# Four blocks of one-hots by one comparison of two repeated sources, eight blocks ahead, in the aggregations of a graph network

## The reference, cut to what matters

```python
m = jax.ops.segment_sum(h[src], dst, num_segments=n) * jax.lax.rsqrt(deg_in)[:, None]   # layer 0
summed = jax.ops.segment_sum(feat[src], dst, num_segments=n)                            # layer 1
out = jax.ops.segment_sum(msg, dst, num_segments=n)                                     # layer 2
```

## Time and profile before

| | |
|---|---|
| median of 3 executions | 7148.84 us (7143.23 to 7172.1) |
| the profiled execution, its own time | 7161.93 us |
| its span, first to last instruction | 7160.4 us |
| the three aggregations in it | 411 to 1469, 2851 to 3910, 4060 to 5116 us |
| busy over the span: PE, DVE, POOL, ACT | 79%, 57%, 52%, 24% |
| granted clock of PE, mean | 0.789 |

### The profile page before, as it was taken

One profiled execution on the slowest core, in us unless ns is written; L12 is line 12 of the kernel. 1 busy time (PEld: TensorE's weight loads), 2 busy tenths in 40 slices (PEclk: granted clock), 3 DMA queues, 4 the chain that ended last, 5 costly groups with the idle time before them and its releaser, 6 DMA issues. The chain is left out here.

```text
span 7160.4 us, 108405 instructions
## 1 busy us (share of the span) xinstructions
PE 5677.4 (79%) x22527; PEld 3639.6 (51%) x22527; DVE 4076.5 (57%) x12903; ACT 1747.1 (24%) x5772; POOL 3739.3 (52%) x4098
## 2 busy tenths in 40 slices
PE   3578878750899945777786688888669999999999
PEld 3444444340688723444443433333357777777777
DVE  8656666671111154555555455555447777777777
ACT  0110000011222202000000200000136666666666
POOL 0157777705322272777775377777414444444442
PEclk9977777755899957777776755556569999999999
DMA  4033333312899821444444233333312222222222
GB/s 194 24 92 106 105 105 105 105 16 60 287 320 321 271 69 46 113 113 113 113 113 88 69 105 105 105 105 105 66 42 71 73 73 73 73 73 73 73 73 71
DMA packets 532967, 771.27 MB, mean 108 GB/s; under 512 B 309632, under 2 KB 371786, under 8 KB 531469
## 3 DMA queue, kind: packets, MB, share of 16 engines
q0 software_dynamic: 198688, 483.47, 24.2%
q1 hardware_dynamic: 288093, 253.58, 11.6%
q10 hardware_dynamic: 45952, 31.72, 1.4%
HBM read 677.13 MB, written 97.84 MB: 108 GB/s over the span
## 5 line engine op out<-in xcount | busy, mean ns | idle before, releaser
L769 PE MATMUL bank<-agg_msg,agg_hot 128*125 128x256 f32 (+1 forms) x4992 | 2328.5, 580 | 636.3 <-DMA agg_msg<-table,agg_idx 397.9
L671 POOL DMA_INDIRECT agg_msg<-table,agg_idx x2496 | 2366.4, 948 | 778.8 <-issue 651.8
L769 PEld LDWEIGHTS bank<-agg_msg,agg_hot 128*125 128x125 f32 x4992 | 1083.3, 262 | 1858.7 <-DVE agg_hot L688 1359.3
L700 DVE TENSOR_TENSOR acc<-acc,bank 125x256 f32 x2496 | 1051.2, 421 | 978.1 <-PE bank L769 964.3
L1604 POOL DMA_INDIRECT tp_src<-table,tp_idx x832 | 790.6, 950 | 1004.6 <-DVE tp_idx L1672 862.4
L1623 ACT ACTIVATE tp_hots<-tp_hot,tp_attr 128x125 f32<-128x125 f32 x3328 | 1047.1, 387 | 0.2 <-issue 0.2
L1685 DVE TENSOR_TENSOR acc<-acc,bank 125x512 f32 x832 | 572.4, 688 | 415.8 <-PE bank L1651 291.8
L688 DVE TENSOR_SCALAR agg_hot<-iota_i,dst_w 128x126 f32<-128x126 f32 x2496 | 736.6, 296 | 0.0
L1651 PEld LDWEIGHTS bank<-tp_msg,tp_hots 128*125 128x125 f32 x4992 | 685.7, 190 | 48.1
L1651 PE MATMUL bank<-tp_msg,tp_hots 128*125 128x128 f32 x4992 | 690.4, 275 | 0.0
L1639 PE MATMUL bank<-tp_fc,tp_hid 64*128 64x256 f32 x1664 | 587.6, 434 | 0.0
(11 more groups left out here) (272 smaller groups left out, 5701.9 us busy)
## 6 DMA issues: line engine op xcount, KB each, us to landing
acc<-in_L_w_laid_dram SPq DMA_DIRECT2D x162, 512.0 KB, 4.3
acc<-in_L_gnn_w_dram SPq DMA_DIRECT2D x162, 512.0 KB, 6.3
agg_msg<-table,agg_idx POOLq DMA_INDIRECT x2496, 2.8
table<-tab_out SPq DMA_DIRECT2D x40, 625.0 KB
token_rows<-prep_zero SPq DMA_DIRECT2D x9, 2304.0 KB
ffn_rows<-token_rows POOLq DMA_DIRECT2D x162, 128.0 KB, 5.0
expert_rows<-ffn_res ACTq DMA_DIRECT2D x162, 128.0 KB, 6.0
tp_scal<-scal_parts SPq DMA_DIRECT2D x832, 18.0 KB
```

The costliest lines, as they stand in the source:

```text
L671: pool.indirect_dma_start(out=msg[PER * g + r][:, 0:D], out_offset=None, in_=table[:, :], in_offset=bass.IndirectOffsetOnAxis(ap=idx[g][:, ...
L700: dve.tensor_tensor(row, row, bank[0:P, 0:D], ALU.add).then_inc(s_add, 1)
L769: pe.matmul(net.bank[w % BANKS][0:P, 0:sums], hot[w % HOTS][:, 0:P], msg[w][:, :], start=True, stop=True).then_inc(s_sum, 1)
```

## The change

`match` now does its work only for every fourth block. One `tensor_tensor` comparison writes the one-hots of four blocks, 4 x 125 columns: its first source is the row 0 to 124, repeated four times, its second the four destination numbers of each partition, each repeated 125 times. Both sources lie in SBUF. The ring is four buffers of four blocks instead of eight of one block, and `match` is called for block w + 8 instead of w + 6; so DVE does it at w = 0, 4, 8 and 12, behind `add(w)` and the index copy. PE waits for the semaphore of the one-hots once per four blocks. Nothing else is changed.

```diff
-HOT_W = 126
@@ aggregate
-    HOTS, HOT_AHEAD = 8, 6
+    HOTS, HOT_AHEAD = 4, 8
-        hot = [ph.sb(f"hot{r}", [Q, HOT_W]) for r in range(HOTS)]
+        hot = [ph.sb(f"hot{r}", [Q, PER, P]) for r in range(HOTS)]
                 def match(i, r):
-                    dve.tensor_scalar(hot[r % HOTS][:, :], net.iota_i[:, 0:HOT_W], net.dst_w[:, ds(WPI * i + r, 1)], None,
-                                      ALU.is_equal).then_inc(s_hot, 1)
+                    if r % PER == 0:
+                        wide = [Q, PER, P]
+                        dve.tensor_tensor(hot[r // PER][:, :, :], bc(net.iota_i[:, 0:P], 1, wide),
+                                          bc(net.dst_w[:, WPI * i + r:WPI * i + r + PER], 2, wide), ALU.is_equal).then_inc(s_hot, 1)
@@ body of PE
-                        pe.wait_ge(s_hot, WPI * i + w + 1)
+                        if w % PER == 0:
+                            pe.wait_ge(s_hot, GROUPS * i + w // PER + 1)
-                        pe.matmul(net.bank[w % BANKS][0:P, 0:sums], hot[w % HOTS][:, 0:P], msg[w][:, :],
+                        pe.matmul(net.bank[w % BANKS][0:P, 0:sums], hot[w // PER][:, w % PER, :], msg[w][:, :],
```

## The result

The changed kernel takes 7241.1 us in the median of 4 runs (7230.2 to 7266.3), the kernel before 7146.0: a ratio of 1.013, with a 95% interval of 1.0093 to 1.0168. It is slower by 95 us. The profiled execution of the changed kernel has a span of 7264.6 us against 7160.4 before.

The account below looks back on a forecast made before the run. POOL's row of gathers was taken to bound the kernel. The lock's +129 us and −5 us for removed comparisons gave +124, 7286 us over the profiled 7161.9; that execution lies 13 us above the median, so 7273, range 7185 to 7335.

Parts of the forecast that it names:

- Part 1: Less work on DVE: 624 comparisons of 678 ns replace 2496 of 296 ns; DVE gives up some 314 us, worth nothing.
- Parts 2 and 3: DVE's new order costs nothing, up to 1 us per aggregation; PE's 1872 dropped waits give nothing to a few us.
- Part 4: Wide comparison with two SBUF sources locks POOL during gathers: 206 ns each, 129 us in all, bounds nothing to 331 us.
- The first place: 0.13 us into a gather, where POOL waits for the comparison's end: share 0.42, mean delay 0.265 us, 111 ns.
- even spread: Comparisons taken to start at a random point of the 1.251 us between gathers; gives 206 ns each, 129 us.
- steady stretch: Gathers at 4500.31 and 4501.56: wide comparison would end 0.26 us into the latter, delay 0.13 us, 81 us over 624.
- The second place: Late in a gather, at 0.86 us, POOL would again wait for the comparison: share 0.39, mean 0.24 us, 95 ns.
- rival B: Only the lock early in the gather counts: 69 us by random positions, 64 net, time 7213 us; chance 0.17.
- A: The forecast itself: locks early and late in the gather both delay POOL; 7273 us, own range 7220 to 7335; chance 0.60.
- Part 5: POOL's gathers, mean 948 against median 946 ns: removing the old comparisons gives back at most 5 us.

Follow-up runs that it names:

- the burst of four: Four short tensor_scalar comparisons of one block each in place of the changed kernel's wide one: 7154.3 us, ratio 1.0010 to the kernel before.

## Why the prediction was right, and where it was not

**What bounds the kernel** was right: POOL's row of gathers. The 90.9 us added to the gathers are 87% of what the span grew, and the three aggregations' gathers start over 1071.7, 1067.3 and 1075.1 us instead of 1041.1, 1041.9 and 1040.3, which is 90.8 more.

**Part 1**: 678 ns were forecast for a comparison, 673 measured. That the saving on DVE is worth nothing was right. Its size was not: DVE's busy time fell by 161 us (4076.5 to 3915.5) and not by 314, though the lengths of all its records added up fell by 335. The records of neighbouring DVE operations overlap: in the earlier trace rows the copy starts 0.34 us after a sum that takes 0.42. Lengths of single records added up over-count the engine's time.

**Parts 2 and 3** were right: POOL's idle time didn't change at all, and the burst of four, with the same order, ring and waits, is at 1.0010.

**Part 4** had the right lock at the gather's start, and two wrong terms that partly made up for each other. The first place was put at 111 ns a comparison, by even spread; it measured 150 ns (93.3 us over 624). 389 of the 624 comparisons, a share of 0.62 and not 0.42, delay a gather at its start. The prediction saw this in its steady stretch, worked out 81 us from it, and chose even spread. The second place was put at 95 ns a comparison and measured none. The step that failed is "L712 started 0.67 us into one and took 0.33, so POOL held the lock then". The timeline of the kernel before shows what I overlooked:

```profile
2905.38 0.52 DVE L688 TENSOR_SCALAR agg_hot<-iota_i,dst_w 128x126 f32<-128x126 f32 x1
2905.57 0.33 DVE L712 TENSOR_TENSOR agg_whole<-agg_whole,agg_part 128x121 f32<-128x121 f32 x1
```

L688 ahead of it was kept waiting (0.52 instead of 0.28), and both end at 2905.90: L712 only stood behind it in the queue. POOL's late hold is against operations of the removed kind; comparisons with two sources don't meet it (14 of 225 against 200 of 203, above). So the mechanism was rival B's, and the time, 7241, lies between B's 7213 and the forecast of 7273, inside A's own range only because the first place cost more. That the number came out well is in part luck.

What the experts' gathers in the earlier trace rows waited for stays open. The prediction read them as L1453's end alone. But two of the fifty L1453 start inside a gather, run far past 0.76 us of it and delay nothing, in the gathers of 2524.56 and 2545.69; in the first it ends 1.09 us in:

```profile
2524.56 1.21 POOL L1435 DMA_INDIRECT take_got<-expert_rows,take_of  x1 [0.30 <-issue]
2525.17 0.49 DVE L1453 SCALAR_TENSOR_TENSOR acc<-take_got,moe_gate,acc 125x256 f32 x1 [0.15 <-DVE acc L1452]
2525.80 0.17 DVE L1446 COPY take_of<-moe_get 125x2 f32 x1 [0.15 <-DVE acc L1453]
```

They differ from the delayed ones in two ways: L1453 starts later (0.61 us into the gather against 0.51 at most), and the two-element copy L1446, of the kind that holds late, starts only behind the gather. In the delayed ones it starts inside it, mostly 0.15 us after L1453's end, so these rows can't tell the two apart; a run that removes the copy was not made.

**Part 5**: 5 us at most were forecast; 2.4 is the gathers' difference between the kernel before and that with the row in PSUM.

## What to carry to other kernels

Where POOL's indirect gathers set the pace, a saving on DVE is worth nothing, and the form of the DVE operations beside them is worth a lot: keep operations with two SBUF sources short or give one source a place in PSUM, and keep one-source f32 copies at the double pace short as well. Here a comparison of 0.28 us cost next to nothing and one of 0.67 us cost 0.15. Fusing four short operations into a long one can cost more than it saves, as the engine behind the lock gets in only between operations. When an operation looks kept waiting in a timeline, look first at the one ahead of it on its own engine.

## What the runs showed of the hardware that I had not expected

A DVE operation of 0.28 us with two SBUF sources costs the gathers 3 ns and one of 1.2 us costs 494 ns. An indirect gather of 125 rows takes 1.20 us of POOL, one of 128 rows 0.946. One session ran the kernel before at 7955 us instead of 7148, with POOL waiting some 700 to 780 us for indices in the two kernels with gathers of 128 rows that were profiled there; the cause is not known. A copy at the double pace has a late place in the gather, at 0.83 us, that comparisons with two SBUF sources don't have.
